# Rank sums copied to SBUF by ScalarE, one activation table, plain probability transposes, in a one-core audio tower kernel

## The reference, cut to what matters

```python
scores, idx = jax.lax.top_k(sim, PK_TOPK)
index = (idx0[..., :, None] + idx1[..., None, :])
score = (scores[0][..., :, None] + scores[1][..., None, :])
final_scores, pk_idx = jax.lax.top_k(score, FINAL_TOPK)
final_scores = jax.nn.softmax(final_scores, axis=-1)
k = jnp.einsum('bnhk,bnhkd->bnhd', kv_scores, keys_table[ind])
v = jnp.einsum('bnhk,bnhkd->bnhd', kv_scores, values_table[ind])
sim = jnp.einsum('bihd,bjhd->bhij', q, k)
attn = jax.nn.softmax(jnp.where(causal, sim, neg), axis=-1)
out = jnp.einsum('bhij,bjhd->bhid', attn, v)
```

## Time and profile before

| | |
|---|---|
| median of three runs | 5672.43 us |
| profiled execution | 5717.41 us |
| its span, first to last instruction | 5715.6 us |
| TensorE, matmuls busy | 4461.4 us, 78% of the span |
| VectorE busy | 4149.2 us, 73% |
| ScalarE busy | 2381.2 us, 42% |
| GpSimd busy | 2630.5 us, 46% |
| granted TensorE clock, mean | 0.932 |

### The profile page before, as it was taken

How to read it: one execution, slowest core, us unless ns; L and a number is a source line. 1 busy time by engine, 2 the same in 40 slices (tenths; PEclk the granted TensorE clock), 3 DMA queues, 4 the chain that set the end, 5 groups by cost and what they waited for, 6 DMA issues and landing times.

```text
span 5715.6 us, 105503 instructions
## 1 busy us (share of the span) xinstructions
PE 4461.4 (78%) x28801; PEld 2922.6 (51%) x28801; DVE 4149.2 (73%) x16693; ACT 2381.2 (42%) x5639; POOL 2630.5 (46%) x2915
## 2 busy tenths in 40 slices
PE   6677772168888888888888888888888888888888
PEld 4555551035555555555555555555555555555556
DVE  4677767558687878787878787878787878787833
ACT  3333331124444444444444444444444444444444
POOL 0011101253555555555555555555555555555551
PEclk8999995579999999999999999999999999999999
DMA  1000002022222323222322232323232323232321
GB/s 43 1 0 0 0 2 57 22 67 72 80 83 84 88 77 91 76 85 80 89 77 86 81 89 77 91 74 90 75 89 76 91 76 94 71 94 74 96 74 57
DMA packets 160562, 389.43 MB, mean 68 GB/s; under 512 B 65847, under 2 KB 69943, under 8 KB 159612
## 3 DMA queue, kind: packets, MB, share of 16 engines
q1 hardware_dynamic: 78876, 215.14, 12.0%
q0 software_dynamic: 81120, 167.81, 11.2%
HBM read 379.87 MB, written 4.61 MB: 67 GB/s over the span
## 4 chain that ended last, share of the span: by engine, by line
DVE 29%; PE 24%; issue 14%; another core or an unknown queue 11%; ACT 4%; DVEq 1%; DMA 0%; ACTq 0%; POOL 0%; POOLq 0%
PE ps L990 24%; DVE w L1656 5%; DVE topi L1461 3%; DVE miss L1587 3%; DVE top L1455 2%; ACT ex L1305 2%; DVE miss L1592 2%; DVE sc L1467 2%; DVE idxf L1626 1%; DVE sm L1666 1%; DVE left L1425 1%; DVE wmat L1646 1%; DVE cs L1467 1%; DVE away L1594 1%
## 5 line engine op out<-in xcount | busy, mean ns | idle before, releaser
L977 POOL DMA_INDIRECT rows<-table_dram,idxT x2528 | 2542.3, 1006 | 2160.3 <-PE ps L990 884.6
L990 PE MATMUL ps<-w,dtab 128*128 128x375 f32 (+1 forms) x6144 | 1814.2, 430 | 6.3 <-issue 5.9
L1656 DVE SCALAR_TENSOR_TENSOR w<-ps,ex 128x750 f32<-128x750 f32 (+1 forms) x1152 | 1108.5, 962 | 917.7 <-ACT ex L1305 366.7
L990 PEld LDWEIGHTS ps<-w,dtab 128*128 128x128 f32 x6144 | 1047.3, 199 | 392.8 <-issue 80.0
L1305 ACT ACTIVATE ex<-ps 128x750 f32<-128x750 f32 (+1 forms) x1152 | 946.7, 822 | 550.6 <-PE ps L990 367.1
L990 PE MATMUL ps<-rank_dense,half 128*128 128x375 bf16 (+1 forms) x2432 | 563.6, 323 | 377.8 <-DVE w L1656 299.4
L990 PE MATMUL ps<-parts,half 128*128 128x375 bf16 x2176 | 561.7, 341 | 193.9 <-ACT ex L1305 152.3
L990 PEld LDWEIGHTS ps<-rank_dense,half 128*128 128x128 bf16 x2432 | 207.5, 100 | 854.0 <-DVE w L1656 524.4
L491 POOL COPY states<-n_h 64x32 f32 (+1 forms) x375 | 76.7, 205 | 750.6 <-DVE n_h L480 750.6
L382 PE MATMUL ps<-which,bias 128*64 128x256 bf16 (+2 forms) x3123 | 397.5, 280 | 8.7 <-DVE which L461 8.7
L990 PEld LDWEIGHTS ps<-parts,half 128*128 128x128 bf16 x2176 | 208.2, 108 | 366.9 <-ACT ex L1305 198.7
(11 more groups left out here) (223 smaller groups left out, 6666.0 us busy)
## 6 DMA issues: line engine op xcount, KB each, us to landing
dtab<-dense_dram SPq DMA_DIRECT2D x256, 512.0 KB
dtab<-corner_dram SPq DMA_DIRECT2D x128, 512.0 KB
rows<-table_dram,idxT POOLq DMA_INDIRECT x2528
xin<-x_dram SPq DMA_DIRECT2D x16, 187.5 KB
early<-early_dram SPq DMA_DIRECT2D x1, 1800.5 KB, 9.2
half<-halves_dram POOLq DMA_DIRECT2D x1, 1680.0 KB, 12.7
rows_in<-hh SPq DMA_DIRECT2D x16, 93.8 KB, 2.2
rows_in<-uu SPq DMA_DIRECT2D x16, 93.8 KB, 2.2
```

What stands on the lines that cost most here:

```text
L977: nc.gpsimd.indirect_dma_start(out=rows[:, PLACES[u] * GROUP + j, :], out_offset=None, in_=table[:, :], in_offset=bass.IndirectOffsetOnAxi ...
L990: return nc.tensor.matmul(out_, lhsT, rhs, start=start, stop=stop, skip_group_check=open_bank)
L1656: nc.vector.scalar_tensor_tensor(w[:, p % 2, :, 0:wide], ps[:, 2:4, 0:wide], float(K), ex[:, p % 2, :, 0:wide], ALU.is_lt, ALU.mult).then_ ...
```

## The change

ScalarE's step gets one more instruction: behind Exp(p) it waits for `s_D` of step p and copies the rank sums out of banks 2 and 3 into `rank_sum`, one of two bf16 SBUF buffers (`s_rs`). `ranks` of the next step waits for that copy instead of w. VectorE's w waits for Exp and the copy and reads `rank_sum` instead of PSUM. The rank sums and the threshold are whole numbers.

In the softmax the scaled identity goes; ScalarE multiplies `prob` in place by the reciprocal sums, and TensorE turns the blocks with its transpose instruction. At the start of the attention part ScalarE loads one table set that is to serve Exp and Ln both.

```diff
+        rank_sum = sb("rank_sum", [128, 2, 2, 2 * CH * TT], BF16)
...
-        dg = sb("dg", [TT, 2, TT])
...
+        s_rs = sem("d_rank_sum_copied")
...
             def ranks(n, p):
                 if not (isinstance(n, int) and n == 0 and p == 0):
-                    pe.wait_ge(s_w, n * STEPS + p)
+                    pe.wait_ge(s_rs, n * STEPS + p)
...
-                pe.wait_ge(s_dg, count(n, m) + 1)
+                pe.wait_ge(s_pn, count(n, m) + 1)
                 for j in range(c + 1):
-                    last = mm(ps[0:TT, 6, j * TT:(j + 1) * TT], prob[:, m % 2, j * TT:(j + 1) * TT], dg[:, m % 2, :])
+                    last = nc.tensor.transpose(ps[0:TT, 6, j * TT:(j + 1) * TT], prob[:, m % 2, j * TT:(j + 1) * TT], ident[0:TT, 0:TT])
...
                 nc.scalar.activation(ex[:, p % 2, :, 0:wide], ps[:, 0:2, 0:wide], ACT.Exp).then_inc(s_ex, 1)
+                act.wait_ge(s_D, n * STEPS + (p + 1))
+                nc.scalar.copy(rank_sum[:, p % 2, :, 0:wide], ps[:, 2:4, 0:wide]).then_inc(s_rs, 1)
...
-            def scaled_identity(m, n):
+            def normalise(m, n):
+                J = (ITEMS[m][1] + 1) * TT
                 act.wait_ge(s_ri, count(n, m) + 1)
-                nc.scalar.activation(dg[:, m % 2, :], ident[0:TT, 0:TT], ACT.Copy, scale=mx[:, 2, m:m + 1]).then_inc(s_dg, 1)
+                nc.scalar.activation(prob[:, m % 2, 0:J], prob[:, m % 2, 0:J], ACT.Copy, scale=mx[:, 2, m:m + 1]).then_inc(s_pn, 1)
...
+            nc.scalar.preload_act_table_set("natural_log_exp_and_others")
             run(act, front, promote, nothing, step)
...
             def weight(n, p):
-                dve.wait_ge(s_D, n * STEPS + (p + 1))
                 dve.wait_ge(s_ex, n * STEPS + (p + 1))
+                dve.wait_ge(s_rs, n * STEPS + (p + 1))
                 wide = T if p < CORNER else 2 * CH * TT
-                nc.vector.scalar_tensor_tensor(w[:, p % 2, :, 0:wide], ps[:, 2:4, 0:wide], float(K), ex[:, p % 2, :, 0:wide],
+                nc.vector.scalar_tensor_tensor(w[:, p % 2, :, 0:wide], rank_sum[:, p % 2, :, 0:wide], float(K), ex[:, p % 2, :, 0:wide],
                                                ALU.is_lt, ALU.mult).then_inc(s_w, 1)
```

More of the change, by code:

```diff
@@ L848, in attention @@
         s_av, s_aq = sem("c_vout_product"), sem("c_q_product")
-        s_s, s_e, s_ri, s_dg, s_tp = (sem(n) for n in ("c_sim", "c_exp", "c_sum_inverted", "c_scaled_identity", "c_probs_turned"))
+        s_s, s_e, s_ri, s_pn, s_tp = (sem(n) for n in ("c_sim", "c_exp", "c_sum_inverted", "c_probs_scaled", "c_probs_turned"))
         s_o, s_osb, s_out = sem("c_out_summed"), sem("c_out_copied"), sem("c_out_stored")
@@ L1366, in step @@
                 for m in items(TURN_AT, p, kind):
-                    scaled_identity(m, n)
+                    normalise(m, n)
                 for m in items(SIM_AT, p - 2, kind):
```

## The result

Over seven runs the changed kernel takes **5711.20 us** in the median (5697.48 to 5730.44), the kernel before in the same rounds 5672.87 us: a ratio of 1.0075, 95% interval 1.006 to 1.0091. The change costs 0.75%, some 42 us; the two medians alone, which don't pair the runs, are 38 us apart. I had forecast 5636 us and faster; the time lies inside the range, the sign was wrong.

A forecast was written before the change was run, and what follows sets the result against it. Two bounds alternate in each of 16 sequences: VectorE in the front stretch (steps 10 to 65), TensorE in the bare stretch (66 to 9). +70 - 80 - 12 - 14 = -36 off 5672.4 gave 5636 us, range 5540 to 5760.

The forecast's parts named there:

- plain transposes: TensorE's turns of prob: 768 fewer records, only those of 8 blocks a bare stretch count, -14 us; ends 0 and -85.
- table loads: ScalarE: 94 loads of 1.283 us go, 121 us, mostly covered by front work; a tenth taken, -12 us; ends 0 and -121.
- extra copy: ScalarE: 1152 copies of 822 ns, 947 us; at 59% of the span, in bulk nothing while TensorE and VectorE cover it.
- the lead: TensorE's rank matmuls no longer wait for w, running at most one step ahead: 5.0 us a sequence, -80 us; ends 0 and 138.
- The latency: Between rank matmuls and w, copy plus semaphore cost 0.87 us at five waits a sequence: 4.4 us, +70 us.
- I take half of 7.2: Lead in the front stretch: half of VectorE's 7.2 us wait won; sims' shared banks and gathered units eat the rest.
- all of 1.4: Lead at the start of the bare stretch: all of TensorE's 1.4 us wait for w is won.
- It just fits, so 0: Bare stretch: TensorE's 2.2 us from rank matmul to product covers the 1.9 us of copy, w and semaphores, so no cost.
- The latency case: Rival, front stretch between s_D and w: the copy's latency outweighs the lead, +113 us, 5785 us; chance 0.22.
- Full lead: Rival: front stretch loses its 7.2 us, bare one its 1.4, copy hidden by the lead; -164 us, 5508 us; chance 0.15.
- nothing: Rival: waits gone come back at the next one, transposes and loads were hidden; 5665 us, within noise; chance 0.13.
- The gathers were held up: Rival, GpSimd: w's two SBUF sources delay gathers starting under it; +80 us if gathered units come late, 5716 us; chance 0.08.

The follow-up runs named there:

- Mask first: The changed kernel with VectorE's mask of a sim moved ahead of w in its step: ratio 1.0036 to the kernel before.
- the kernel without the lead: The changed kernel with the rank matmuls waiting for w again as well as for the copy: ratio 1.0194 to the kernel before.
- doubled transposes: Each of the 768 transposes issued twice, in the changed kernel without the copy (1.0009) and in the changed kernel (1.0065).
- the product: Blocks turned by a plain-identity product, two records each, instead of transposes, in the changed kernel without the copy (1.0011) and in the changed kernel (1.0057).
- filler: Unused TensorE work put ahead of its waits, two versions each: in the kernel before 1.0054 and 1.0041, in the changed kernel 1.0066 and 1.0053.
- without the copy: The changed kernel without the rank-sum copy: w straight from PSUM, ranks waiting for w, one table set and plain transposes kept; ratio 1.0040 to before.
- the copy that nobody reads: The changed kernel, but ScalarE's copy is of a constant into an unread buffer; w reads PSUM and ranks wait for w: ratio 1.0069 to before.

## Why the prediction was wrong

The steps that failed are the plain transposes, put at -14 us with 0 as the worst end (alone they cost 21), the table loads, -12 us (measured +2), the extra copy, put at 0 (measured +16), and 13 us of the lead. The latency, the largest term, was right.

Each rung of this ladder is one edit on top of the one above it, in us of 5672:

| step | forecast | measured | good to |
|---|---|---|---|
| transposes and table set | -26 | +23 | 6 |
| ScalarE busy with one more copy | 0 | +16 | 13 |
| w behind that copy | +70 | +71 | 15 |
| TensorE's lead | -80 | -67 | 14 |
| sum | -36 | +43 | 9 |

*Latency of w: right.* Five waits of 0.87 us a sequence; 71 us in the ratio and 68 in w's idle time. The term also holds w's new source and the slower gathers, which the run doesn't part from it.

*Lead of TensorE: right in kind, 13 us too large.* The step "I take half of 7.2" had named what eats it, the shared banks. What I had not priced is that these cost more pieces than sims: values, flips and queries queue behind a mask in the same bank, 132 us of idle time before the values alone. Mask first gave back 22 us of it. By the traces the size that failed is "all of 1.4": against the kernel without the lead the front stretch is 4.3 to 4.8 us shorter (I had 3.6), but the bare one is 0.5 to 1.0 us longer, whether the steps are cut at w, at the product or at Exp.

*Plain transposes: the step that failed.* I let 8 blocks of the bare stretch count at -14 us and set the worst end at 0; that they could cost time I left out, for no reason. Alone they cost 0.37%, 21 us. The time saved was real, TensorE's busy time at the turns fell from 254.4 to 173.5 us, but TensorE idles as long before them as before (123.6 against 128.0 us), and in the last 50 us, where it would have counted, the clock fell to half. That accounts for some 8 of the 21 us; the rest stays open. The Trainium skill (TensorE: Matmul & The Clock Gate, section "Part 4: PE-mode transpose") says that transposes don't count as work for the clock the way matmuls do. No run here bears that out: behind the last w doubled transposes had a mean clock of 0.91 and 0.92 in two kernels, the product 0.86 and 0.79.

*Table loads: nothing instead of -12 us alone, -21 with the copy.* "I take a tenth" was a guess between 0 and 121; it was a term that depends on another one. The 94 loads are hidden as long as ScalarE has room. For the same reason the preload is the one part of the change that pays in it.

*The extra copy "in bulk nothing": failed, +16 us.* A share of 55% hides in bulk, but not at each step. Which steps is not settled. I first looked at the bare stretch, where I had written "It just fits, so 0". Mean over 14 sequences from w(66) to w(10) of the next, one profile each: 57.8 to 61.1 us in the six kernels without that copy and without filler or early mask (before and without the copy: 59.3), 60.8 to 62.0 in the six with it (changed 61.8, the copy that nobody reads 61.2). But w marks a place on VectorE, and what TensorE does between two such marks is not the same: 132 product matmuls in the kernel before, 144 in the changed one, and TensorE idles 11.0 and 11.2 us. Cut at the start of Exp, the stretch takes 63.3 us before and 63.0 changed, 62.6 without the copy and 63.4 with the one that nobody reads. So a part of the 2 us is work that changed sides. The front stretch went from 225.3 to 223.3 us cut at w and from 221.3 to 222.1 cut at Exp; the sign that I had named for being wrong, over 5 us, did not show, and the forecast was wrong all the same. The execution traced of before was also 45 us above its median, 2.8 us a sequence, more than any of these differences.

*w from SBUF: right*, 965 against 962 ns.

*The rivals.* The latency case had the sign right and the reason wrong: the latency cost no more than forecast; the loss came from the turns and from the fuller ScalarE. Full lead and "nothing" are out. **The gathers were held up**, as that rival said; the price that I put on it isn't seen, and whatever they cost is inside the 71 us of the latency. Of the gathers that start under a w, 601 of before took 0.95 us in the mean, 438 of the changed kernel 1.27, with up to 1.96. Its timeline, a w and a gather that ends after twice its usual time:

```profile
4245.10 1.19 DVE L1661 SCALAR_TENSOR_TENSOR w<-rank_sum,ex 128x1000 f32<-128x1000 bf16 x1
4245.15 1.96 POOL L978 DMA_INDIRECT rows<-table_dram,idxT  x1 [0.31 <-issue]
```

In the kernel with the copy that nobody reads, where w reads PSUM, the mean is back:

```profile
L977 POOL DMA_INDIRECT rows<-table_dram,idxT x2528 | 2528.7, 1000 | 2181.2 <-PE ps L990 1019.6 <-issue 693.8 <-DVE w L1660 211.6
```

So it is w's second SBUF source, and not ScalarE's traffic. It adds 118 us to an engine that idles 2034.

## What to carry to other kernels

A stage moved to a third engine costs its latency where the next engine stands idle, and that term could be read off the trace here (70 forecast, 71 measured); the lead that it gives ends at the next shared buffer, so look at who frees each bank before counting it. Work taken off an engine that then waits all the same gains nothing: give such a term a bound above zero too, and look at the end of the kernel, where nothing hides the engine and a sparser stream can leave it at half clock. A cost hidden beside an engine's idle time (table loads here) is not a constant, it comes due when the same change fills that engine.

## What was not expected of the hardware

- With one record a block instead of two, TensorE's clock stayed at 0.50 for 31 to 52 us on end behind the last w in the nine traces with single transposes, though TensorE was busy 10.45 of 12 us in one such stretch; with two records it was back after at most 10.2 us.
- Mean granted clocks of 0.933 and 0.953 went with 5678 and 5701 us: the clock is no measure of how good a kernel is.
- A copy of 750 columns took 788 ns from PSUM, f32 to bf16, and 820 ns from SBUF, bf16 to bf16: the narrower source gave ScalarE no time.
- The mask ahead of w cost 0.28% in the kernel before and gave 0.39% in the changed one: edits of this size do not add up in this kernel, where three engines meet several times in a step. Each is little above what a difference of two ratios can tell, so a term below 20 us should be measured in the kernel it is meant for.
